# Softmax epilogue cut into steps and spread over the next query block in an 8-core attention and mixture-of-experts kernel

## The reference

```python
x = x + attn(layernorm(x), Wqkv, bqkv, Wr, br)
x = x + ffn(layernorm(x), shared_up, shared_down, routed_up, routed_down, router_w)
# attn: 16 heads of 64; content = q k^T / 8
#   rp = q Wr^T + br              (257 relative positions)
#   pos[i, j] = rp[i, clip(j - i, -128, 128) + 128]
#   out = softmax(content + pos) v
# ffn: 2 shared experts + 16 routed, top 4 by softmax gate, gelu, width 512
```

## Time and profile before

| what | value |
|---|---|
| median of 2 runs | 5360.88 us (5335.5 and 5386.25) |
| the profiled execution | 5259.77 us |
| span of its slowest core | 5258.2 us (cores 5231.1 to 5258.2) |
| mean granted TensorE clock of that core | 0.792 of full speed |
| TensorE busy | 3255.1 us, 62% of the span |
| VectorE busy | 1946.8 us, 37% |
| ScalarE busy | 1577.8 us, 30% |
| attention stage | from about 1060 us to 3630 us of the span |

### The profile page before, as it was taken

One profiled execution on the slowest core, in us unless ns is written; L12 is line 12 of the kernel. 1 busy time (PEld: TensorE's weight loads), 2 busy tenths in 40 slices (PEclk: granted clock), 3 DMA queues, 4 the chain that ended last, 5 costly groups with the idle time before them and its releaser, 6 DMA issues.

```text
span 5258.2 us, 58340 instructions; the slowest of 8 cores (5231.1 to 5258.2 us)
## 1 busy us (share of the span) xinstructions
PE 3255.1 (62%) x16435; PEld 1050.1 (20%) x16557; DVE 1946.8 (37%) x4059; ACT 1577.8 (30%) x1928; POOL 623.3 (12%) x1152
## 2 busy tenths in 40 slices
PE   1555443166666566666666666786199994179996
PEld 0121111011112111111111111221033331033332
DVE  1122232333333333332423323322644443644444
ACT  1121110134445344354344443565011111011111
POOL 3000000201011020110110101101011111011110
PEclk8887776578778777787787877887599997599998
DMA  6111101101100011010110100002044444034332
GB/s 152 63 49 44 56 24 59 49 9 44 30 31 27 21 45 33 23 32 24 40 37 16 36 27 33 25 1 33 1 60 60 63 63 78 0 47 62 60 62 61
DMA packets 127593, 220.73 MB, mean 42 GB/s; under 512 B 23290, under 2 KB 77050, under 8 KB 126268
## 3 DMA queue, kind: packets, MB, share of 16 engines
q0 software_dynamic: 105408, 187.08, 17.0%
q1 hardware_dynamic: 21884, 29.92, 1.6%
HBM read 235.82 MB, written 63.05 MB: 57 GB/s over the span
## 4 chain that ended last, share of the span: by engine, by line
PE 44%; DVE 18%; DMA 13%; ACT 8%; issue 8%; DVEq 5%; POOL 2%; ACTq 2%; POOLq 0%; SPq 0%
PE PP L247 24%; PE PA L247 6%; DMA rp_hbm<-big 5%; PE PV L247 5%; PE PD L247 5%; DVEq L257 5%; PE PB L247 4%; DVE f32c L263 3%; DMA k_hbm<-bfc 3%; ACT bfc L877 2%; DMA big<-v_hbm 2%; ACTq L260 2%; DVE big L725 1%; ACT big L877 1%; POOL rp_hbm L243 1%
## 5 line engine op out<-in xcount | busy, mean ns | idle before, releaser
L247 PE MATMUL PP<-big 128*128 128x512 bf16 x5262 | 1291.3, 396 | 300.8 <-DVEq L257 113.4
L247 PEld LDWEIGHTS PP<-big 128*128 128x128 bf16 x5376 | 501.2, 100 | 1091.4 <-issue 642.1
L877 ACT ACTIVATE bfc<-PA 128x1024 bf16<-128x1024 f32 x344 | 352.6, 1025 | 686.6 <-PE PA L247 674.2
L1221 DVE TENSOR_TENSOR f32s<-f32s,PP 128x512 f32<-128x512 f32 x544 | 374.3, 688 | 270.2 <-PE PP L247 270.0
L1182 ACT ACTIVATE f32c<-PP 128x512 f32<-128x512 f32 x256 | 153.1, 598 | 913.5 <-PE PP L247 912.7
L247 PE MATMUL PD<-bfc,ones_bf 128*1 128x512 bf16 (+1 forms) x1516 | 363.5, 431 | 77.0 <-ACT bfc L379 49.4
L877 ACT ACTIVATE bfc<-PB 128x1024 bf16<-128x1024 f32 x344 | 352.1, 1024 | 112.6 <-PE PB L247 112.4
L247 PE MATMUL PA<-f32s,big 64*128 64x512 bf16 x1024 | 245.4, 456 | 156.3 <-POOLq L92 77.9
L247 PE MATMUL PV<-bfc,big 128*64 128x512 bf16 x1376 | 313.3, 452 | 0.0
L243 POOL DMA_DIRECT2D big<-wupT x288 | 152.5, 559 | 1293.6 <-PE PD L247 817.5
L247 PE MATMUL PP<-f32s,ones_bf 64*1 64x512 bf16 (+1 forms) x256 | 66.8, 566 | 374.6 <-DVEq L257 374.6
(11 more groups left out here) (176 smaller groups left out, 3241.9 us busy)
## 6 DMA issues: line engine op xcount, KB each, us to landing
big<-wupT POOLq DMA_DIRECT2D x288, 128.0 KB, 5.1
big<-wdnT POOLq DMA_DIRECT2D x144, 256.0 KB, 8.6
rp_hbm<-big POOLq DMA_DIRECT2D x256, 128.0 KB, 2.0
bfc<-rp_hbm POOLq DMA_DIRECT2D x256, 96.0 KB, 2.2
f32s<-xT POOLq DMA_DIRECT2D x64, 256.0 KB, 5.1
x_own<-xT POOLq DMA_DIRECT2D x32, 256.0 KB, 8.4
k_hbm<-bfc SPq DMA_DIRECT2D x64, 128.0 KB, 1.9
v_hbm<-bfc SPq DMA_DIRECT2D x32, 256.0 KB, 2.0
```

The lines of the kernel that those rows point to most:

```text
L247: E.matmul(d, l, r, start=st, stop=sp, tile_position=tp, skip_group_check=True), sem, 1)
L877: sop(lambda E, pa=pa, pc=pc: E.activation(pchunk[pc][:, :], pa[:, 0:1024], AF.Exp))
L1221: v_aa = vop(lambda E, pA=pA, hc=hc, jp=jp: E.tensor_add(acc[:, hc * 1024 + jp * 512:hc * 1024 + (jp + 1) * 512], acc[:, hc * 1024 + jp * ...
```

## The change

Three things are edited.

1. The epilogue becomes seven functions: `ep_copies` (with one drain less between the two copies), four `ep_recip` that each take the reciprocal of 128 of the 512 columns, `ep_cast` (the bf16 split), and `ep_fin` (broadcast, multiply, add). For blocks 0 to 2 they are put into a list, and two of them are issued in each of the next block's first chunks, behind the chunk's QK and ahead of a pending PV: `ep_copies` and the first reciprocal in chunk 0, two reciprocals in chunk 1, the last one and `ep_cast` in chunk 2, `ep_fin` in chunk 3. For block 3 all seven are issued at once, as before.
2. The next block's first PV waits for the mark behind `ep_copies`. The first PV of the next pair waits for the end of the last epilogue (`epil_sems[(ch, 3)]`), where it waited for the mark behind the copies.
3. In `rp_step(0)` and `rp_step(15)` the scratch is `f32s[:, 6144:6656]` in place of T1, since T1 now holds reciprocals while these steps run.

```diff
@@ rp_step, qt 0 and 15
                 for hh in range(2):
-                    vop(lambda E, hh=hh: E.tensor_scalar(
-                        T1[:, 0:512], rpstg2[hh][:, :], scal[:, 24 + hh:25 + hh],
+                    rmt = f32s[:, 6144:6656]
+                    vop(lambda E, hh=hh, rmt=rmt: E.tensor_scalar(
+                        rmt, rpstg2[hh][:, :], scal[:, 24 + hh:25 + hh],
                         None, ALU.subtract))
...
@@ emit_main
-        pv_start_guard = tail["pv_free"]
+        pending_epi = []
+        pv_start_guard_ref = [(None, {"v_pvc": tail["pv_free"]})]
...
                 t_qk = P.mark("tensor", "sPe")
+                for _ in range(2):
+                    if pending_epi:
+                        pending_epi.pop(0)()
                 if len(pending) >= 2:
                     pending.pop(0)()
...
                     if kc == 0:
-                        P.wait("tensor", "sVe", guard)
+                        P.wait("tensor", "sVe", guard["v_pvc"])
...
+            def ep_copies(qblk=qblk, t_last=t_last):
+                P.wait("vector", "sPe", t_last)
+                vop(lambda E: E.tensor_copy(T2[0:65, 0:512], PD[0:65, :]))
+                vop(lambda E: E.tensor_copy(T2[:, 512:1024], PV1[:, :]))
+                vdrain()
+                est["v_pvc"] = P.mark("vector", "sVe")
+
+            def ep_recip(part):
+                c0 = part * 128
+                vop(lambda E, c0=c0: E.reciprocal(T1[0:65, c0:c0 + 128],
+                                                  T2[0:65, c0:c0 + 128]))
+                vdrain()
...
+            ep_steps = [ep_copies] + [lambda p=p: ep_recip(p) for p in range(4)] + \
+                       [ep_cast, ep_fin]
+            if qblk == 3:
+                for f in ep_steps:
+                    f()
+            else:
+                pending_epi.extend(ep_steps)
+            pv_start_guard_ref[0] = (qblk, est)
...
-                    "pv_free": pv_start_guard}
+                    "pv_free": epil_sems[(ch, 3)]}
```

More of the change, by code:

```diff
@@ L896, in den_pv @@
                 def den_pv(i=i, kc=kc, pc=pc, s_e=s_e, v_cp=v_cp, q0=q0,
-                           guard=pv_start_guard):
+                           guard=pv_start_guard_ref[0][1]):
                     P.wait("tensor", "sSc", s_e)
@@ L915, in emit_main @@
             t_last = pvden_done[qblk * NKC + NKC - 1]
-            P.wait("vector", "sPe", t_last)
-            vop(lambda E: E.tensor_copy(T2[0:65, 0:512], PD[0:65, :]))
-            vdrain()
-            vop(lambda E: E.tensor_copy(T2[:, 512:1024], PV1[:, :]))
-            vdrain()
-            v_pvc = P.mark("vector", "sVe")
-            recip_nr(T1[0:65, 0:512], T2[0:65, 0:512], T1[0:65, 512:1024])
-            vop(lambda E: E.tensor_copy(rcbf[0:65, :], T1[0:65, 0:512]))
-            vdrain()
@@ new lines, in ep_recip, with ep_cast @@
+            def ep_recip(part):
[3 more added lines that the diff above has]
+                vdrain()
+                if part == 3:
+                    P.mark("vector", "sVe")
+            def ep_cast():
+                vop(lambda E: E.tensor_copy(rcbf[0:65, :], T1[0:65, 0:512]))
+                vdrain()
+                vop(lambda E: E.tensor_sub(rclo[0:65, :], T1[0:65, 0:512],
+                                           rcbf[0:65, :]))
+                vdrain()
+                est["v_rc"] = P.mark("vector", "sVe")
@@ new lines, in ep_fin @@
+            def ep_fin(ch=ch, qblk=qblk, q0=q0):
+                b = pp_next()
+                P.wait("tensor", *ppfree[b])
+                P.wait("tensor", "sVe", est["v_rc"])
+                mm(PP[b][0:64, :], ones_bf[0:1, 0:64], rcbf[0:1, :], True, False)
+                mm(PP[b][64:128, :], ones_bf[64:65, 0:64], rcbf[64:65, :], True, False,
+                   tp=(64, 64))
+                mm(PP[b][0:64, :], ones_bf[0:1, 0:64], rclo[0:1, :], False, True)
+                mm(PP[b][64:128, :], ones_bf[64:65, 0:64], rclo[64:65, :], False, True,
+                   tp=(64, 64))
+                t_bc = P.mark("tensor", "sPe")
+                P.wait("vector", "sPe", t_bc)
+                vop(lambda E, b=b: E.tensor_mul(T1[:, 512:1024], T2[:, 512:1024],
+                                                PP[b][:, :]))
+                vdrain()
+                v_pvf = P.mark("vector", "sVe")
+                ppfree[b] = ("sVe", v_pvf)
+                if ch == 0 and qblk == 0:
+                    P.wait("vector", "sXl", x_own_ld)
+                vop(lambda E, ch=ch, q0=q0: E.tensor_add(
+                    x_own[:, ch * 2048 + q0:ch * 2048 + q0 + 512],
+                    x_own[:, ch * 2048 + q0:ch * 2048 + q0 + 512], T1[:, 512:1024]))
+                vdrain()
+                epil_sems[(ch, qblk)] = P.mark("vector", "sVe")
@@ L954, in emit_main @@
+            ep_steps = [ep_copies] + [lambda p=p: ep_recip(p) for p in range(4)] + \
[6 more added lines that the diff above has]
+            pv_start_guard_ref[0] = (qblk, est)
+        while pending_epi:
+            pending_epi.pop(0)()
         while steps:
```

38 lines of the change are left out of this document (5 added, 33 removed).

## The result

The changed kernel takes 5176.39 us, median of 11 runs (5164.06 to 5302.97); the kernel before, run beside it on the same chip, 5335.93 us, median of 10 (5252.87 to 5386.26). The ratio is 0.9865, with a 95% interval from 0.9801 to 0.9929. The gain is 1.35%, about 71 us, and the interval goes from 37 to 105 us. The slowest core's span in the profiled execution went from 5258.2 to 5162.5 us, mean granted clock about 0.80 after 0.792. So the change is a gain, just under what counts as more than 2%.

The account below looks back on a forecast made before the run. No engine is full; waits of one engine for another bound the attention stage. Terms: 7 x (3.4 + 1.2 + 2.8) = 51.8, plus 12, less 5, 59 us off 5360.88, giving 5302 us; range 5195 to 5375 us.

Parts of the forecast that it names:

- A part costs 955 ns: VectorE in the epilogue: a reciprocal of 128 columns takes 955 ns, 1.03 us with its drain.
- The chain longer by 0.63 us: VectorE's epilogue chain: four parts take 4.14 us against 3.43 for one; with one drain saved, 0.63 us longer.
- a small reciprocal has a high floor: Rival, slower: at 1.67 us per part all 32 epilogues lose, 32 us slower, 5393 us; chance 0.06.
- Seam 0, 3.4 us: Behind block 0 in seven pairs with steps: the add of rp_step(1) at 1507.2 in place of 1510.61, 3.4 us each.
- Seam 1, 1.2 us: Behind block 1 in seven pairs: band_step(1) and QK of chunk 4 earlier by 0.8 to 1.4, taken as 1.2 us.
- Seam 2, 2.8 us: Behind block 2 in seven pairs: QK of chunk 4 3.2 us earlier, less 0.4 for the clock, 2.8 us.
- Last pair, 4.0 us: Three seams without steps: QK of chunk 4 4.5 us earlier, less 0.5 for the low clock; 12 us in all.
- Behind block 3, a loss of 5 us: Eight ends of pairs, nothing spread: the 0.63 us longer chain is a pure cost, 5 us in all.
- The clock: TensorE at the seams: some 3.5 us of idling is left, so most drops stay and move to chunk 3.
- about 1 us more each: Last pair's seams: if idling were short enough to keep 2.4 GHz, each would give about 1 us more.
- no change: Rival: steps set the pace of blocks 1 to 3, only the last pair counts, 7 us, 5354 us; chance 0.17.
- All waits vanish: Rival, faster by over 2%: waits ahead of the 24 spread broadcasts vanish, 217 us less 5, 5149 us; chance 0.12.

Follow-up runs that it names:

- the lengthened chain: Three more subtractions with their drains in each epilogue's split, 2.3 us more ahead of each broadcast, against the changed kernel: 5261.72 us, ratio 1.0002.
- free PV: Changed kernel, but a chunk without band copies no longer makes its PV wait for the newest VectorE mark: 5181.21 us, ratio 0.9842; with one reciprocal 5155.56 us, 0.9803.

## Why the prediction was right and where its terms were off

The direction, the mechanism and the class were right: faster by less than 2% (ratio 0.9865). The sum was too small: 59 us against 86 us on core 4's exponentials (87.6 on the mean of eight cores). With a ratio so near the 2% line, that the class came out as forecast owes something to luck. The absolute forecast, 5302 us, is no test of the mechanism, and the result lies 19 us below the low end of the range, 5195 us. It was put against the median of two executions, 5360.88 us, and the ratio rests on 5259.65 us for the kernel before; against the profiled execution of 5259.77 us the same sum gave 5200.8, and 5188.57 was measured. Term by term:

- **A part costs 955 ns**: 949 measured. The chain longer by 0.63 us: 0.54, because the first part starts 1.41 us behind the copies (1688.52 to 1689.93) where the prediction had 1.5. The rival that a small reciprocal has a high floor is out. The Trainium skill's rule of a fixed latency per VectorE instruction ("VectorE: DVE Perf Modes", the section on the TRN2 errata) made three more instructions 0.47 us, by an estimate; the trace agrees, with 0.45 us (4 x 949 less 3349 ns).
- **Seam 0, 3.4 us**: the add of `rp_step(1)` was forecast 17.3 us behind the copies (1507.2 less 1489.88) and came 17.1 us behind; the blocks gained 3.5. Right, and for the reason given: the fourth part and the split behind `rp_step(0)`, POOL no longer last.
- **Seam 1, 1.2 us**: 3.1 measured on core 4, 2.6 on the mean of eight cores. The broadcast was forecast at 10.6 us behind the copies and came at 10.2; QK of chunk 4 was forecast at 13.1 (1598.0 less 1584.94) and came at 12.5. That far the working held, a little on the low side. The step that failed is to end it at QK of chunk 4, as the place where the stage is back in its pace. ScalarE's list has the exponential of `band_step(1)` ahead of chunk 4's, and it waits for VectorE's second add. Before, that add was the end of a chain over VectorE and ScalarE: first add, exponential of `band_step(0)`, exponentials of chunks 2 and 3, second add. The first add moved from 10.8 to 6.6 us behind the copies (forecast: 7.0), since the multiply and the add of the epilogue no longer stand ahead of it, and this chain with it. The second add is now held by the broadcast and the bank behind it, at 13.2 us in place of 15.5. The exponential of chunk 4 gains as much as the second add: over all 56 seams it came 18.05 us behind the copies and comes 15.82 behind them, 2.2 us. A further 0.4 us comes later in the block. That the gain is seam 1's own is shown by spreading seam 1 alone, and that the split's place sets the end of the changed chain by the lengthened chain (2.2 us of 2.3 at this seam, mean of eight cores); that the old chain went over ScalarE is read from the rows and the lists, and no run takes that exponential away.
- **Seam 2, 2.8 us**: 3.9 measured. QK of chunk 4 was forecast at 10.2 us behind the copies and came at 10.3, a gain of 3.1 us; what was wrong is the 0.4 us that I took off for the clock. The rest of the block did not lose, but gained another 0.7 on average. On the mean of eight cores the exponentials of chunks 4 to 9 are 3.1 to 3.2 us earlier and from chunk 15 on 3.8 to 3.9. Which wait gives that up stays open.
- **Last pair, 4.0 us**: 3.5 on average (3.1, 4.8, 2.6). QK of chunk 4 came 4.75 us earlier where 4.5 was worked out, but the low clock behind the wait cost more than my 0.5 us.
- **Behind block 3, a loss of 5 us**: the broadcast is later by the 0.54 us, and yet the blocks behind a pair's end are not longer (112.0 and 111.6). In the kernel with pieces cut and not spread the same stretch was 113.7 on core 4 and 111.8 and 112.0 on two others. On the mean of eight cores it is 112.5 before, 112.9 cut and not spread, and 111.9 in the changed kernel: the cost of cutting shows at 0.4 us, and something in the changed kernel gives back 1 us that no run isolates. I should have given the term from 0 to 5 us.
- **The clock**: I expected the drops to stay, and they did. Of the last pair's blocks the granted clock was 0.93 to 0.96 after 0.86 to 0.93, and it became 1.00 in all three only in the kernels where the idling was 0.28 us. What I had taken from "TensorE: Matmul & The Clock Gate" of the Trainium skill (Part 1, on the HAM clock gate), that seams with short idling would keep the high level, is borne out by that kernel, and it was worth more than the "about 1 us more each": a block fell from 44.8 to 39.8 us, of which 3.35 us is the wait (3.63 less the 0.28 that is left) and the other 1.6 us goes with the clock (that kernel also has one reciprocal and free PV).
- **The rivals**: no change is out, since the stage is 86 us shorter and each seam contributes. "All waits vanish" is out for the changed kernel, whose waits are still 216.8 us. That VectorE's chain at the seam counts in full is what the lengthened chain shows.

What I had not asked: whether the change's placement was a good one. The prediction listed for each seam what stands on VectorE's list between the pieces, and at seam 0 that was already the reason for an 11 us wait; the better order follows from the same list.

## What to carry to other kernels

When a chain is spread over later work, each seam has its own last arrival: follow every ring (add, stores, next add at seam 0; add, exponentials, next add at seam 1) to where it closes, and do not stop at the first engine that looks free. Check the releaser that a profile names against the order of the lists: of several semaphores it names the one that came last, which need not be one that the instruction needed. When a shorter chain brings nothing, look at which other instruction has inherited the wait; waits on "the newest mark" of an engine are dependencies that no data needs, and they surface once something long is put ahead of them. Choose the place of the pieces seam by seam, because one schedule that is best where nothing else runs holds a shared buffer too long where something does.

## What was not expected of the hardware

TensorE's clock did not answer to equal idling in equal ways. With four parts and the broadcast in chunk 5, TensorE was idle for 2.45 us at each of the last pair's three seams. On core 6:

```profile
3378.50:3420.97 42.47, 38.64 (x268) 10.40 (x266) 10.54 (x35) 32.55 (x32) 0.00 (x0) 1.00 0.00 1
3420.97:3466.01 45.04, 41.52 (x268) 10.63 (x266) 10.66 (x35) 32.65 (x32) 0.00 (x0) 0.92 0.01 1
```

The same instructions and the same wait of 2.45 us (in front of PV of chunk 2, the false wait again) stand in both blocks. In the first the granted clock stayed at 1.00, in the second it fell to the lower level for a while, and that block took 2.6 us more. On core 4 all three blocks had the drop (0.92, 0.89 and 0.92; 44.8, 46.2 and 45.0 us). Over all eight cores, 17 of the 24 blocks had it and 7 had not: each core but core 4 was spared once, in its first or second block. So a wait's price here is its length plus a drop that may or may not come, 0 or from 2.2 to 4.0 us at a wait of 2.45 us, and single blocks are not to be compared. Behind waits of 0.28 us the clock did not fall in any of the 72 blocks of three kernels (two of them, on cores 0 and 1 of one kernel, began below full speed from before the seam). Behind 3.63 us it was below full speed in all 48 of the last pair's blocks in the changed kernel's two traces.
